# Reordering VectorE and ScalarE work between two batches' key tiles in a gated cross-attention kernel

## What is computed

```
h   = layernorm(x)                       # per row, 512 features
q   = h @ Wq.T + bq                      # 16 heads of 32
k   = ctx @ Wk.T + bk;  v = ctx @ Wv.T + bv
att = softmax(q k^T / sqrt(32) + mask)   # 100 x 722 for each head
x1  = x + tanh(g0) * ((att v) @ Wo.T + bo)
n   = layernorm(x1)
p   = softmax(n @ gate_w + gate_b)       # 8 experts: the router's sums
out = x1 + tanh(g1) * sum over the two largest p of p_e * expert_e(n)
```

## Time and profile before

| | |
|---|---|
| median of 3 runs | 1775.42 us (1775.21 to 1775.77) |
| the profiled execution's own time | 1774.65 us |
| its span, first to last instruction | 1772.8 us |
| mean granted TensorE clock | 0.998 of full speed |
| TensorE busy | 1752.1 us, 99% of the span |
| VectorE busy | 1243.0 us, 70% |
| ScalarE busy | 953.4 us, 54% |
| GpSimd busy | 184.0 us, 10% |

### The profile page before, as it was taken

The page is one execution under the profiler, slowest core; times in us unless marked ns, Lnnn a source line. Parts: engine busy times, 40 slices in busy tenths (PEclk is TensorE's granted clock), DMA queues, the critical chain, the costliest instruction groups (busy, mean ns, idle before and its releaser), DMA issues.

```text
span 1772.8 us, 39866 instructions
## 1 busy us (share of the span) xinstructions
PE 1752.1 (99%) x14694; PEld 1517.1 (86%) x14694; DVE 1243.0 (70%) x3382; ACT 953.4 (54%) x1780; POOL 184.0 (10%) x271
## 2 busy tenths in 40 slices
PE   9999999999999999999999999999999999999997
PEld 8888888888888888888888877877899999999996
DVE  5677777778777777877776556666677777777772
ACT  4655656565555556565655544545555555545551
POOL 1110110111011001101100010000000111111110
PEclk9999999999999999999999999999999999999999
DMA  8982232222122222222204399998666666767661
GB/s 265 382 314 67 80 86 69 72 80 81 53 79 85 67 66 81 86 70 71 76 29 146 103 328 395 360 350 302 216 208 207 205 210 208 218 219 219 219 195 37
DMA packets 123229, 292.68 MB, mean 165 GB/s; under 512 B 17859, under 2 KB 36291, under 8 KB 123088
## 3 DMA queue, kind: packets, MB, share of 16 engines
q1 hardware_dynamic: 99664, 225.46, 37.8%
q0 software_dynamic: 23424, 65.30, 12.8%
HBM read 244.04 MB, written 46.66 MB: 164 GB/s over the span
## 4 chain that ended last, share of the span: by engine, by line
PE 95%; DMA 2%; DVE 1%; issue 1%; ACT 1%; POOL 0%; DVEq 0%; SPq 0%; ACTq 0%; POOLq 0%
PE bank_rows L2364 21%; PE bank_rows L727 16%; PE bank_rows L713 15%; PE bank_rows L775 8%; PE bank_rows L2379 6%; PE bank_rows L765 5%; PE bank_rows L786 4%; PE bank_rows L2418 4%; PE bank_rows L2445 3%; PE bank_rows L2404 3%; PE bank_rows L750 3%; PE bank_rows L802 3%; PE bank_rows L865 2%; DMA stage<-in_L_ffn_w 1%; PE bank_rows L789 1%; PE bank_rows L851 1%
## 5 line engine op out<-in xcount | busy, mean ns | idle before, releaser
L1177 ACT ACTIVATE probs<-probs,neg_max 100x722 f32<-100x722 f32 x248 | 221.0, 892 | 107.5 <-DVE neg_max L1528 107.5
L1521 DVE CUSTOM_DVE_ANT_0 probs<-bank_rows,mask_sb 100x362 f32<-100x362 f32 x496 | 234.4, 529 | 6.9 <-PE bank_rows L765 6.6
L2608 DVE TENSOR_TENSOR w_low<-stage,w_high 128x1024 fp32r<-128x1024 f32 x176 | 213.1, 1222 | 36.4 <-ACT w_high L2512 35.8
L1182 ACT ACTIVATE p_t<-bank_rows 121x600 f32<-121x600 f32 x256 | 171.3, 669 | 68.9 <-PE bank_rows L775 66.5
L2512 ACT ACTIVATE w_high<-stage 128x1024 fp32r<-128x1024 f32 x176 | 183.5, 1056 | 34.3 <-DMA stage<-in_L_ffn_w 34.1
L2535 ACT ACTIVATE gelu<-bank_rows,biases 128x256 f32<-128x256 f32 x176 | 82.1, 473 | 220.3 <-PE bank_rows L2364 186.6
L2364 PE MATMUL bank_rows<-h_low,w_high 128*128 128x256 f32 x704 | 199.2, 283 | 0.0
L2364 PE MATMUL bank_rows<-h_high,w_low 128*128 128x256 f32 x704 | 199.2, 283 | 0.0
L2364 PE MATMUL bank_rows<-h_high,w_high 128*128 128x256 f32 x704 | 199.2, 283 | 0.0
L713 PE MATMUL bank_rows<-ctx_high,wk_high 128*128 128x360 f32 (+1 forms) x512 | 182.7, 357 | 4.8 <-DVE k_low L1494 3.5
L775 PE MATMUL bank_rows<-ident,probs 100*121 100x100 f32 x1488 | 180.8, 257 | 1.3 <-ACT p_t L1182 1.3
(11 more groups left out here) (250 smaller groups left out, 3835.6 us busy)
## 6 DMA issues: line engine op xcount, KB each, us to landing
stage<-in_L_ffn_w SPq DMA_DIRECT2D x240, 512.0 KB, 4.5
plain_w<-in_L_ffn_w SPq DMA_DIRECT2D x15, 2048.0 KB, 12.2
expert_in_rows<-filling POOLq DMA_DIRECT2D x8, 3341.0 KB, 20.3
router_rows<-in_gate_rows POOLq DMA_DIRECT2D x112, 200.0 KB, 3.4
ctx_raw<-in_ctx SPq DMA_DIRECT2D x16, 720.0 KB, 4.5
ctx_raw<-in_ctx SPq DMA_DIRECT2D x15, 724.0 KB, 4.4
xs_sb<-expert_in_rows SPq DMA_DIRECT2D x11, 514.0 KB, 5.2
b_sb<-in_L_ffn_b SPq DMA_DIRECT2D x19, 256.0 KB
```

Of the source, the lines that this page charges most:

```text
L1177: nc.scalar.activation(p, p, ACT.Exp, bias=neg_max[:, h:h + 1], scale=-1.0, accum_out=exp_sum[:, h:h + 1]).then_inc(probs_ready, 1)
L1182: nc.scalar.activation(p_t[:, h % HQ, :, :].rearrange("t (k i) s -> t k (i s)", k=2), bank_rows[0:TT, 4:6, 0:3 * S], ACT.Copy).then_inc(pt ...
L1521: nc.vector.tensor_tensor_reduce(out=probs_of(b, g)[:, q, at], in0=score_bank[q][0:S, 0:size], in1=mask_sb[:, at], scale=-1.0, scalar=BIG, ...
L2608: nc.vector.tensor_tensor(lo, src, hi.bitcast(F32), ALU.subtract).then_inc(chunk_lo[which], 1)
```

## The change

Three places. In VectorE's odd bodies the first of the router's sums moves in front of `queries_low`, the second stays behind it, and the third moves behind `keys_low` of tile 0, half 0. In ScalarE's first body `rstd_start(0, 2)` moves behind the copies of heads 10 and 11. In VectorE's first body `recips(b, 2)` moves in front of `ln_apply(0, 2, ...)`. TensorE's, GpSimd's and SyncE's lists, the unit lists and the counts of all instructions stay as they are.

```
@@ ScalarE, first_body
             keys_high(b, n, 2, 0)
-            rstd_start(0, 2)
             copy_probs(b, 10)
             copy_probs(b, 11)
+            rstd_start(0, 2)
             keys_high(b, n, 0, 1)
@@ VectorE, first_body
             keys_low(b, n, 2, 0)
+            recips(b, 2)
             ln_apply(0, 2, x_ln[:], xn[:], xn_ready)
-            recips(b, 2)
             keys_low(b, n, 0, 1)
@@ VectorE, body
             if odd:
+                dots(t, (0,))
                 queries_low(b, "Q23")
-                dots(t, (0, 1, 2))
+                dots(t, (1,))
                 keys_low(b, n, 0, 0)
+                dots(t, (2,))
             else:
                 keys_low(b, n, 0, 0)
                 dots(t, (0, 1, 2))
```

## The result

| | before | after |
|---|---|---|
| median of 18 runs each | 1775.01 us (1774.36 to 1777.96) | 1771.84 us (1771.08 to 1773.74) |
| the profiled execution's own time | 1774.65 us | 1771.73 us |
| its span | 1772.8 us | 1769.9 us |

The ratio is 0.9982 with a 95% interval of 0.9976 to 0.9989: 3.2 us faster, and just within the 0.2% that was called "same". The forecast median was 1772.5 us; of the 0.7 us between it and 1771.84, 0.4 is that three runs of the kernel before had put its median at 1775.42 and eighteen put it at 1775.01. The profiled executions differ by 2.92 us, the sum forecast 2.94 us.

What follows compares the result with a forecast made beforehand. TensorE, busy 99% of the span, was taken as the bound. 1774.65 - 3.0 (7 x 0.43) + 0.06 = 1771.7 us for a profiled execution; forecast median 1775.42 - 2.94 = 1772.5 us, range 1770.5 to 1774.8.

Steps and rivals of the forecast that it cites:

- First sum in front of the queries at no cost: VectorE, odd bodies: the sum starts at 243.33 inside the 0.95 us idle hole; queries' low part stays at 244.28.
- K00's low part at 246.44: VectorE, odd bodies: key tile's low part waits only for ScalarE, starting at 246.44 instead of 247.22.
- The stall of 0.66 us is gone: TensorE, odd bodies: K20 may start at 247.09, before 247.21 when it can start at all; 0.12 us to spare.
- The next wait, L765 for `half_max`: TensorE, odd bodies: group 2's second-half scores wait for maxima until 249.62; 0.23 us comes back, 0.43 us stays.
- Nothing more lost later in the body: Odd bodies: second half's maxima at 250.94, 0.46 us earlier; head 8's exponential has 0.35 us to spare.
- GpSimd's loads cost nothing: Odd bodies: first sum's load issues 1.7 us earlier, third's about 0.3 us later, wanted seven and more us later.
- First body +0.06 us: First body: the copies' 0.43 us gain is given back at group 3's maxima, leaving it 0.06 us longer.
- The full stall is won: Rival, odd bodies: maxima do not hold group 2's second-half scores; 4.6 us gain, 1770.9 us; chance 0.13.
- GpSimd holds the low part: Rival, odd bodies: GpSimd's load issue delays K00's low part to 246.87; no gain, 1775.5 us; chance 0.08.
- The first sum waits in front of the queries: Rival, odd bodies: late router rows delay the sum and queries' low part; 2.1 us slower, 1777.5 us; chance 0.05.
- Given back elsewhere: Rival: an unfound wait behind group 2 takes half the gain; 1774.0 us; chance 0.08.
- rival H: In the seventh kernel: transfers stand behind the fills in the same queue, so early loads land no earlier than 129 to 131.

Runs made afterwards that it cites:

- third experiment: Changed kernel's odd order, but second and third sums both between queries and K00's low part, first body as before the change: 1770.14 us, ratio 0.9973.
- shifted kernel: The changed kernel with 24 more semaphore increments at the start of VectorE's list and nothing else: 1772.09 us, ratio 0.9984.
- seventh kernel: The sixth kernel with GpSimd waiting for the fills before its first scatter instead of before the first router loads: 1769.11 us, ratio 0.9967.
- sixth kernel: Third experiment's odd order, reciprocals before `ln_apply`, and head 10's copy before the key tile's high part and inverse deviation: 1769.32 us, ratio 0.9968.
- fourth: Changed kernel's odd order, but first two sums behind the queries, only the third behind K00's low part; first body as before: 1771.67 us, ratio 0.9983.
- fifth: Changed kernel's odd order, but second and third sums both between K00's low part and the maxima; first body as before: 1777.44 us, ratio 1.0013.

## Why the forecast held, step by step

1. *First sum in front of the queries at no cost.* Right. It starts at 243.25 (forecast 243.33) and the queries' low part is unmoved at 244.28. In body 1 too it had to wait for nothing. It also turned out to be unnecessary, which no step said: two sums fit between the queries' and the key tile's low parts.
2. *K00's low part at 246.44.* Right to the hundredth.
3. *The stall of 0.66 us is gone.* Right in kind, but the stall was taken too small. K20 starts 0.34 us behind XT, where the step took 0.40 us from the even body. By the third experiment the full stall is 3.92 - 3.18 = 0.74 us. Why the two units start closer here than in an even body, no run shows.
4. *First maximum at 247.57, last read ends at 249.47.* 247.56 and 249.46.
5. *The next wait, L765 for `half_max`.* Right, and it sets what the change is worth: forecast 249.62, measured 249.60. Forecast 0.23 us back and 0.43 kept; measured 0.28 back and 0.46 kept. The mis-sized term is the natural distance of step 3; both sides of the difference move with it.
6. *Nothing more lost later in the body.* Right in bodies 3, 11 and 13 (in body 3 the second half's maxima start at 250.93, forecast 250.94), wrong in body 1.
7. *GpSimd's loads cost nothing.* Wrong in body 1, where two sums waited for their rows (below), right elsewhere.
8. *First body +0.06 us.* Right: +0.07, and +0.06 with that part alone. `ln_apply` at 78.22 (78.24), key tile at 79.32 (79.33), scores at 81.87 (81.89). The reciprocals were covered, and still are: 1.59 us of idle time stands in front of `ln_apply`.

**The sum, again.** Seven bodies at 0.46 us are 3.22 us, not 3.0. Body 1 gives 0.40 back, bodies 7 and 9 keep 0.35 and 0.28 less. Against that, bodies 5 and 8 gain 0.16 and about 0.36 that come from where VectorE's late starts fall (below), not from shorter waits. With body 0, -3.22 + 0.40 + 0.63 - 0.52 + 0.07 = -2.64 us, measured -2.67. The forecast had neither the losses, 0.40 + 0.63 = 1.03 us, nor the gains: 0.22 us more from its seven bodies, 0.52 in bodies 5 and 8 and 0.24 in the experts' part, 0.98 us in all. So "7 x 0.43" was right as a total and describes three bodies out of seven.

**The rivals.** *The full stall is won* fell: the second wait is there, 0.21 us idle. The third experiment shows what it would have been, and its rule: take the sum away from behind the key tile. *GpSimd holds the low part* fell. In body 3 an issue ran from 246.27 to 246.85 and the low part started at 246.44 with its usual 0.59 us. The prediction held that the Trainium skill ("SBUF — State Buffer", "Who interferes with whom"), read strictly, would make this rival. It would not: the section speaks of VectorE instructions with two SBUF inputs, and the low part takes one tensor from SBUF, `k_high`, and the other from PSUM. What the traces show is that such an issue held neither the low part nor, before, the router's sum at 246.60. *The first sum waits in front of the queries* fell, in all seven bodies; but its reason, fills and the router's rows in body 1, did bite, at another place. *Given back elsewhere* was right in part: it had 1.5 us in mind, and 0.40 us (body 1) is what is shown.

## What had not been expected

**Body 1 gives its gain back to the router's loads.** VectorE in body 1 of the changed kernel waits for two sums' rows:

```profile
131.94 0.69 DVE L1586 CUSTOM_DVE_ANT_0 x_res<-x,router_rows 100x512 f32<-100x512 f32 x1 [0.21 <-DMA router_rows<-in_gate_rows]
...
133.76 0.69 DVE L1586 CUSTOM_DVE_ANT_0 x_res<-x,router_rows 100x512 f32<-100x512 f32 x1 [1.13 <-DMA router_rows<-in_gate_rows]
```

GpSimd asked for them only when the fills of the experts' memory had landed. The changed kernel, and then the kernel before:

```profile
128.48 2.40 POOL L530 DMA_DIRECT2D router_rows<-in_gate_rows  x4 [24.70 <-DMA expert_in_rows<-filling]
```

```profile
127.28 1.78 POOL L530 DMA_DIRECT2D router_rows<-in_gate_rows  x3 [23.56 <-DMA expert_in_rows<-filling]
```

VectorE in the old order comes later and does not notice: with the first body's order alone the loads began at 128.40, and no sum waited. ScalarE's exponential of the router and, behind it, its copies are then late for TensorE's transposes. How much is lost depends on when the rows land, and that differs from execution to execution. With the third sum alone moved behind, the loads started at 127.72, no sum waited and body 1 kept its 0.46 us. In the shifted kernel they started at 127.69, no later, but the last ones landed over 1 us later than there: two sums waited 0.49 and 0.63 us, and body 1 kept 0.11 us. So the end of the fills alone does not settle it; what slowed those transfers is not shown. With GpSimd's wait for the fills moved behind its first loads (the seventh kernel), VectorE finds the rows. The rows of sums 4 and 5, then GpSimd's first load:

```profile
130.81 0.69 DVE L1587 CUSTOM_DVE_ANT_0 x_res<-x,router_rows 100x512 f32<-100x512 f32 x1
...
131.65 0.69 DVE L1587 CUSTOM_DVE_ANT_0 x_res<-x,router_rows 100x512 f32<-100x512 f32 x1
```

```profile
122.45 0.55 POOL L530 DMA_DIRECT2D router_rows<-in_gate_rows  x1 [19.28 <-DVE logits L1587]
```

That load landed 6.2 us later, at 128.69; rival H was right that loads issued among the fills are slow. But the rows were there before sums 4 to 7 wanted them. Body 1 keeps 0.76 us, where the sixth kernel kept 0.07. Here the cause is shown.

**Some instructions start late, and it hangs on their place in the engine's list.** The key tile's low part starts 0.11 us after ScalarE's high part. In body 7 of the changed kernel it did not. ScalarE, VectorE:

```profile
487.87 0.56 ACT L1153 ACTIVATE k_high<-bank_rows,bk_sb 128x362 fp32r<-128x362 f32 x1 [1.03 <-PE bank_rows L713]
```

```profile
488.89 0.59 DVE L1494 SCALAR_TENSOR_TENSOR k_low<-bank_rows,bk_sb,k_high 128x362 fp32r<-128x362 f32 x1 [1.14 <-ACT k_high L1153]
```

ScalarE ended at 488.43, VectorE started 0.46 us later, 0.35 us more than usual, which is what body 7 lacks (3.81 - 3.46). With VectorE's list shifted by 24 places and the same work, the same row is

```profile
488.55 0.59 DVE L1494 SCALAR_TENSOR_TENSOR k_low<-bank_rows,bk_sb,k_high 128x362 fp32r<-128x362 f32 x1 [0.79 <-ACT k_high L1153]
```

In body 9 the late one is on ScalarE, whose list was not shifted, and there the shift changed nothing: both kernels show 1.31 us of idle time before it, body 3 has 1.03. The changed kernel, then the shifted one:

```profile
609.52 0.56 ACT L1153 ACTIVATE k_high<-bank_rows,bk_sb 128x362 fp32r<-128x362 f32 x1 [1.31 <-PE bank_rows L713]
```

```profile
609.23 0.56 ACT L1153 ACTIVATE k_high<-bank_rows,bk_sb 128x362 fp32r<-128x362 f32 x1 [1.31 <-PE bank_rows L713]
```

Counting each engine's instructions in the trace from 0, those that only wait for a semaphore included, body 7's late one is number 1471 on VectorE and body 9's 831 on ScalarE. Both leave 63 when divided by 128. In the attention of the kernel before there are 12 starts that come over 0.25 us after everything they are seen to wait for and have as much idle time in front of them; 10 of them leave 63 too, and come 0.32 to 0.48 us after the last thing waited for in their list. Most other instructions at such places follow the one before them at once and show no gap. One of the ten cost the kernel before 0.36 us in body 8, where VectorE started 0.51 us after ScalarE ended at 563.76 + 0.56 = 564.32:

```profile
564.83 0.59 DVE L1494 SCALAR_TENSOR_TENSOR k_low<-bank_rows,bk_sb,k_high 128x360 fp32r<-128x360 f32 x1 [0.81 <-ACT k_high L1153]
```

In the changed kernel, whose list is longer by then, number 1727 is a wait that held nobody up. Body 8 is 0.34 to 0.38 us shorter in every kernel here with a longer list on VectorE, and unchanged (-0.01 us) with the first body's order alone, whose list has the old length.

Body 5 fits as well. In the kernel before, number 1087 is a key tile's low part behind 0.57 us of idle time:

```profile
372.76 0.60 DVE L1494 SCALAR_TENSOR_TENSOR k_low<-bank_rows,bk_sb,k_high 128x362 fp32r<-128x362 f32 x1 [0.57 <-ACT k_high L1153]
```

It stands in front of the second half's maxima, which start 1.70 us after that half's scores (1.35 in body 3), and from those scores to group 3 body 5 takes 11.40 us, the other odd bodies 11.24. In the changed kernel number 1087 follows the instruction before it at once; the maxima start after 1.32 us, and body 5 takes 11.24 us like the rest. In the fourth and fifth kernels number 1087 is a router's sum behind 0.34 us of idle time: maxima after 1.67 us, 11.36 and 11.37 us. In the third, sixth and seventh the same sum is as late, but the maxima still start after at most 1.50 us, and the body takes 11.22 to 11.24. So the late start costs time only where it uses up the slack of the exponential behind these maxima.

That the place in the list decides is shown by the shift: with it body 7's late start is gone, and in body 12 number 2495, a low part, starts 0.17 us after the read that it starts with in the changed kernel. What the engine does at those places is not shown. A late start matters most where a wait is on TensorE's path, as here, and the late starts were there before as well: the one in body 9 was hidden behind the sums. The reordering moved VectorE's because its extra waits made the list longer.

**What stays open.** Whether the order of the seventh kernel could be shifted so that no late start hits bodies 7 and 9, worth 0.3 us each, no run here tells.

## What to carry to other kernels

Work that fills idle time in front of a released bank is free only as long as it ends before the bank could be emptied: count how many pieces fit, put the others where another hole is, and not between the bank and the next thing the bound engine waits for (0.28 us a body for one sum there, 1.11 for two). After each wait removed, compute when the next one ends; here that gave the result to a few hundredths, where the size of the idle entry alone would have promised more. And look at each repetition by itself: the total was right while one body in seven gave its gain back to a late load and two lost much of theirs to a late start. A reordering that adds only waits is not neutral either: it moves every later instruction to another place in its engine's list.
